# Beginning the first block of an attention kernel by two tiles instead of four

## The reference

```python
xn = layernorm(x)
q = (xn @ Wq + bq) / sqrt(256); k = xn @ Wk + bk; v = xn @ Wv + bv
w = softmax(where(causal, q @ k.T, -inf))
x = x + (w @ v) @ Wo + bo
h = layernorm(x); h_prev = h shifted down by one row, zeros on top
r  = sigmoid((mu_r * h + (1 - mu_r) * h_prev) @ W_r)
kk = relu((mu_k * h + (1 - mu_k) * h_prev) @ W_k) ** 2
out = x + r * (kk @ W_v)
```

## Time and profile before

| | |
|---|---|
| median of 3 executions | 365.44 us (364.97 to 365.71) |
| profiled execution | 365.21 us, of it 363.2 us span |
| TensorE busy (matmuls) | 353.2 us, 97% of the span |
| VectorE, ScalarE, GpSimd busy | 254.8, 239.2, 209.0 us |

### The profile page before, as it was taken

How to read it: one execution, slowest core, us unless ns; L and a number is a source line. 1 busy time by engine, 2 the same in 40 slices (tenths; PEclk the granted TensorE clock), 3 DMA queues, 4 the chain that set the end, 5 groups by cost and what they waited for, 6 DMA issues and landing times.

```text
span 363.2 us, 6783 instructions
## 1 busy us (share of the span) xinstructions
PE 353.2 (97%) x2466; PEld 324.5 (89%) x2466; DVE 254.8 (70%) x569; ACT 239.2 (66%) x467; POOL 209.0 (58%) x246
## 2 busy tenths in 40 slices
PE   8999999999999999999999999999999999999995
PEld 6788888989899888899998989999999999989885
DVE  4597888698946786855568876786857558673645
ACT  2355543987659547597565679587368877789572
POOL 4013330468777743579644357678155768699781
PEclk9999999999999999999999999999999999999999
DMA  7600000000012003003000000030000000000001
GB/s 214 220 2 1 2 0 3 0 3 1 2 38 79 1 0 117 1 2 90 28 3 0 2 0 3 29 88 1 3 29 31 0 3 2 30 31 0 31 29 58
DMA packets 11905, 10.64 MB, mean 29 GB/s; under 512 B 1889, under 2 KB 11874, under 8 KB 11874
## 3 DMA queue, kind: packets, MB, share of 16 engines
q1 hardware_dynamic: 10512, 10.23, 8.8%
q10 hardware_dynamic: 1362, 0.01, 0.2%
HBM read 6.04 MB, written 4.19 MB: 28 GB/s over the span
## 4 chain that ended last, share of the span: by engine, by line
PE 76%; DVE 8%; POOL 6%; ACT 5%; issue 3%; DMA 1%; SPq 0%; ACTq 0%; DVEq 0%
PE W L794 16%; PE W L797 16%; PE W L798 15%; PE O L961 7%; PE O L963 7%; PE O L962 7%; PE W L830 3%; POOL kT_hi L364 3%; DVE mix L710 2%; DVE h_row L696 1%; POOL mix_lo L369 1%; DMA h_row<-in_L_attn_Wq_dram 1%; DVE st L675 1%; ACT mix L471 1%; ACT st L416 1%
## 5 line engine op out<-in xcount | busy, mean ns | idle before, releaser
L364 POOL TENSOR_TENSOR p_lo<-st,p_hi 128x512 fp32r<-128x512 f32 (+1 forms) x71 | 80.9, 1157 | 38.8 <-ACT p_hi L416 37.7
L663 DVE TENSOR_TENSOR peak<-peak,W 128x512 f32<-128x512 f32 (+3 forms) x70 | 42.2, 603 | 47.9 <-ACT st L416 47.7
L416 ACT ACTIVATE st<-W 128x512 f32<-128x512 f32 (+1 forms) x79 | 42.5, 538 | 42.3 <-PE W L798 42.2
L961 PE MATMUL O<-v_hi,p_hi 128*128 128x258 f32 x241 | 69.1, 287 | 0.2 <-DVE x_in L685 0.2
L963 PE MATMUL O<-v_hi,p_lo 128*128 128x258 f32 x241 | 68.0, 282 | 0.0
L962 PE MATMUL O<-v_lo,p_hi 128*128 128x256 f32 x241 | 67.7, 281 | 0.0
L797 PE MATMUL W<-xT_lo,kT_hi 128*128 128x512 f32 (+2 forms) x188 | 65.9, 350 | 0.0
L794 PE MATMUL W<-xT_hi,kT_hi 128*128 128x512 f32 (+2 forms) x188 | 64.4, 343 | 0.8 <-DVE kT_lo L573 0.8
L798 PE MATMUL W<-xT_hi,kT_lo 128*128 128x512 f32 (+2 forms) x188 | 63.2, 336 | 0.0
L452 ACT ACTIVATE st<-st 128x512 f32<-128x512 f32 (+1 forms) x79 | 44.8, 567 | 8.7 <-DVE st L675 8.6
L416 ACT ACTIVATE p_hi<-st 128x512 fp32r<-128x512 f32 (+1 forms) x71 | 40.4, 569 | 15.3 <-PE O L963 13.4
(11 more groups left out here) (138 smaller groups left out, 824.3 us busy)
## 6 DMA issues: line engine op xcount, KB each, us to landing
out_dram<-gate SPq DMA_DIRECT2D x15, 256.0 KB, 2.1
x_in<-in_L_attn_y_all_dram SPq DMA_DIRECT2D x7, 512.0 KB, 4.5
x_in<-in_L_attn_y_all_dram SPq DMA_DIRECT2D x2, 256.0 KB, 4.8
h_row<-in_L_attn_Wk_dram SPq DMA_DIRECT2D x1, 256.0 KB, 3.1
h_row<-in_L_attn_Wq_dram SPq DMA_DIRECT2D x1, 256.0 KB, 4.3
st<-in_L_attn_Wv_dram SPq DMA_DIRECT2D x1, 256.0 KB, 5.3
st<-in_L_attn_Wo_dram SPq DMA_DIRECT2D x1, 256.0 KB, 5.5
mix<-in_L_ffn_W_k_dram SPq DMA_DIRECT2D x1, 256.0 KB, 6.6
```

The source lines that it names most:

```text
L364: g.tensor_tensor(lo[:, r], score_tile(u), hi[:, r].bitcast(f32), ALU.subtract).then_inc(p_split, 1)
L416: a.activation(dst, src, ACT.Copy, **kw).then_inc(done, 1)
L663: v.tensor_tensor(peak[:, J % 2, r], peak[:, J % 2, r], scores, ALU.max).then_inc(maxed, 1)
L961: mm(o[:, 0:VW], hi[:, r], v_hi[:, j + b, :], start=j + b == 0, stop=False)
```

## The change

It touches the start alone (and two counts of semaphores that the slots wait for).

- The layer norm of block 0 releases its first two tiles by themselves: the constant 1 is written, and `xhat_ready` raised, after tile 1 and again after tile 3.
- `first_xT(i)` transposes two tiles of `xhat`, both halves of the channels (4 transposes), into one bank. `first_xT(0)` comes right behind the fold, then Wv's transposes, then `first_xT(1)`.
- `xT_hi` and `xT_lo` of block 0 are written by halves of the queries (256 of them, all channels) instead of by halves of the channels. The size of each instruction stays 128x512.
- The key projection of block 0 is done for 256 queries and then for the other 256: 24 matmuls of 256 columns instead of 12 of 512.
- The fold of `wkq` begins with the first half of its contraction as soon as the first half of `wqT` is there (`q_taken` is raised by each half), and its two halves of the result lie in two banks (`folded`). `wkq_hi` and `wkq_lo` are written as two instructions of 256 columns each instead of one of 512.
- `IDLE` goes from (6, 1, 5, 6, 1) to (6, 1, 3, 0, 0): nine products of zeros fewer.

```diff
-    IDLE = (6, 1, 5, 6, 1)
+    IDLE = (6, 1, 3, 0, 0)
...
+        folded = (bank_b, early[0])
...
             for d in range(KC):
-                last = a.activation(wqT[:, d, 1:C], early[1][:, d * C + 1:(d + 1) * C], ACT.Identity, bias=minus_first[:, d:d + 1])
-            last.then_inc(q_taken, 1)
-
-            sc.wait_ge(fold_ready, 3)
-            high(wkq_hi[:], pairs(bank_b), fold_moved, scale=SCALE)
+                a.activation(wqT[:, d, 1:C], early[1][:, d * C + 1:(d + 1) * C], ACT.Identity, bias=minus_first[:, d:d + 1]).then_inc(q_taken, 1)
+
             for h in range(KC):
-                xT_part(0, h)
+                sc.wait_ge(fold_ready, 3 + h)
+                high(wkq_hi[:, h, :], folded[h][:, 0:C], fold_moved, scale=SCALE)
+            for i in range(2):
+                sc.wait_ge(xT_ready, i + 1)
+                high(xT_hi[:, 0, :, i * 2 * P:(i + 1) * 2 * P], pairs(bank_of("xT", 0, i)), xT_high)
...
-                if t == TG - 1:
-                    dve.wait_ge(xhat_done, TG * (G + 1))
-                    v.memset(xhat[:, :, 0:1], 1.0).then_inc(xhat_ready, 1)
+                if t == TG - 1 or G == 0 and t == 1:
+                    dve.wait_ge(xhat_done, TG * G + t + 1)
+                    v.memset(xhat[:, t - 1 if G == 0 else 0:t + 1, 0:1], 1.0).then_inc(xhat_ready, 1)
...
-            dve.wait_ge(fold_moved, 1)
-            v.scalar_tensor_tensor(wkq_lo[:], bank_b[:].rearrange("p (k c) -> p k c", k=KC), SCALE,
-                                   wkq_hi[:].bitcast(f32), ALU.mult, ALU.subtract).then_inc(fold_split, 1)
             for h in range(KC):
-                xT_part(0, h)
-            taken(early[2], wvT, 4, 1)
+                dve.wait_ge(fold_moved, h + 1)
+                v.scalar_tensor_tensor(wkq_lo[:, h, :], folded[h][:, 0:C], SCALE, wkq_hi[:, h, :].bitcast(f32), ALU.mult, ALU.subtract)                    .then_inc(fold_split, 1)
+            for i in range(2):
+                c = slice(i * 2 * P, (i + 1) * 2 * P)
+                dve.wait_ge(xT_high, i + 1)
+                low(xT_lo[:, 0, :, c], bank_of("xT", 0, i)[:].rearrange("p (k c) -> p k c", k=KC), xT_hi[:, 0, :, c], xT_split)
+            taken(early[2], wvT, 5, 1)
...
+            def first_xT(i):
+
+                pe.wait_ge(xhat_ready, i + 1)
+                for h in range(KC):
+                    for t in range(2):
+                        last = nc.tensor.transpose(bank_of("xT", 0, i)[:, (2 * h + t) * P:(2 * h + t + 1) * P], xhat[:, 2 * i + t, h * P:(h + 1) * P], ident[:])
+                last.then_inc(xT_ready, 1)
+
...
-            pe.wait_ge(q_taken, 1)
-            for h in range(KC):
-                for d in range(KC):
-                    last = mm(bank_b[:, h * C:(h + 1) * C], wkT[:, d, h * P:(h + 1) * P], wqT[:, d, :], start=d == 0, stop=d == KC - 1)
-            last.then_inc(fold_ready, 1)
+            for d in range(KC):
+                pe.wait_ge(q_taken, d + 1)
+                for h in range(KC):
+                    last = mm(folded[h][:, 0:C], wkT[:, d, h * P:(h + 1) * P], wqT[:, d, :], start=d == 0, stop=d == KC - 1)
+                    if d == KC - 1:
+                        last.then_inc(fold_ready, 1)
             idle(IDLE[3])
-            for h in range(KC):
-                xT(0, h)
+            first_xT(0)
             pe.wait_ge(wv_loaded, 16)
             transposed(raw_v, early[2])
+            first_xT(1)
             idle(IDLE[4])
...
-            pe.wait_ge(fold_moved, 1)
-            for w, x, done in ((wkq_hi, xh, xT_high), (wkq_lo, xh, fold_split), (wkq_hi, xl, xT_split)):
-                for k in range(KC):
-                    pe.wait_ge(done, 1 if done is fold_split else k + 1)
-                    for h in range(KC):
-                        last = mm(bank_of("kT", 0, h)[:], w[:, k, h * P:(h + 1) * P], x[:, k, :], start=x is xh and w is wkq_hi and k == 0,
-                                  stop=x is xl and k == KC - 1)
-                        if x is xl and k == KC - 1:
-                            last.then_inc(kT_ready, 1)
+            for i in range(2):
+                c = slice(i * 2 * P, (i + 1) * 2 * P)
+                for w, x, done in ((wkq_hi, xh, xT_high), (wkq_lo, xh, fold_split), (wkq_hi, xl, xT_split)):
+                    for k in range(KC):
+                        if done is fold_split:
+                            pe.wait_ge(done, k + 1)
+                        else:
+                            pe.wait_ge(fold_moved, k + 1)
+                            pe.wait_ge(done, i + 1)
+                        for h in range(KC):
+                            last = mm(bank_of("kT", 0, h)[:, c], w[:, k, h * P:(h + 1) * P], x[:, k, c], start=x is xh and w is wkq_hi and k == 0,
+                                      stop=x is xl and k == KC - 1)
+                            if x is xl and i == 1 and k == KC - 1:
+                                last.then_inc(kT_ready, 1)
```

More of the change, by code:

```diff
@@ L531, in _ @@
             for d in range(KC):
-                last = a.activation(wqT[:, d, 1:C], early[1][:, d * C + 1:(d + 1) * C], ACT.Identity, bias=minus_first[:, d:d + 1])
-            last.then_inc(q_taken, 1)
-            sc.wait_ge(fold_ready, 3)
-            high(wkq_hi[:], pairs(bank_b), fold_moved, scale=SCALE)
+                a.activation(wqT[:, d, 1:C], early[1][:, d * C + 1:(d + 1) * C], ACT.Identity, bias=minus_first[:, d:d + 1]).then_inc(q_taken, 1)
             for h in range(KC):
-                xT_part(0, h)
+                sc.wait_ge(fold_ready, 3 + h)
[3 more added lines that the diff above has]
+                high(xT_hi[:, 0, :, i * 2 * P:(i + 1) * 2 * P], pairs(bank_of("xT", 0, i)), xT_high)
             for h in range(KC):
                 kT_part(0, h)
-            sc.wait_ge(fold_ready, 5)
+            sc.wait_ge(fold_ready, 6)
             high(wvo_hi[:], pairs(early[0]), fold_moved)
@@ L634, in _ @@
                 ln1_apply(0, t)
-            dve.wait_ge(fold_moved, 1)
-            v.scalar_tensor_tensor(wkq_lo[:], bank_b[:].rearrange("p (k c) -> p k c", k=KC), SCALE,
-                                   wkq_hi[:].bitcast(f32), ALU.mult, ALU.subtract).then_inc(fold_split, 1)
             for h in range(KC):
-                xT_part(0, h)
-            taken(early[2], wvT, 4, 1)
+                dve.wait_ge(fold_moved, h + 1)
[5 more added lines that the diff above has]
+            taken(early[2], wvT, 5, 1)
             for h in range(KC):
                 kT_part(0, h)
-            dve.wait_ge(fold_moved, 2)
+            dve.wait_ge(fold_moved, 3)
             low(wvo_lo[:], early[0][:].rearrange("p (k c) -> p k c", k=KC), wvo_hi[:], fold_split)
@@ L831, in transposes @@
                 return last
+            def first_xT(i):
[4 more added lines that the diff above has]
+                last.then_inc(xT_ready, 1)
             def xT(G, h):
                 free("xT", G, h)
-                pe.wait_ge(xhat_ready, G + 1)
+                pe.wait_ge(xhat_ready, G + 2)
                 transposes(bank_of("xT", G, h), xhat, h, range(TG)).then_inc(xT_ready, 1)
@@ L840, in kT @@
                 pe.wait_ge(xT_split, KC * (G + 1))
-                if G == 0:
-                    pe.wait_ge(fold_split, 1)
                 project(bank_of("kT", G, h)[:], wkq_hi, wkq_lo, slice(h * P, (h + 1) * P),
@@ L849, in vv @@
                 if G == 0:
-                    pe.wait_ge(fold_split, 2)
+                    pe.wait_ge(fold_split, 3)
                 by_rows(bank_of("v", G, i), range(2 * i, 2 * i + 2), xT_hi[:, G % NT], xT_lo[:, G % NT], wvo_hi, wvo_lo).then_inc(v_ready, 1)
```

## The result

The changed kernel takes 363.27 us (median of 4, 363.17 to 363.32) beside 365.56 us for the kernel before (median of 4, 364.97 to 365.71): ratio 0.994, 95% interval 0.9923 to 0.9957, so faster by 0.4 to 0.8%. Its profiled execution took 363.31 us with a span of 361.2 us, against 365.21 and 363.2. The gain is about 2.0 us by the spans and 2.3 us by these medians; 1.0 was forecast. In the later comparisons, with 21 to 25 executions each, the kernel before has medians of 365.28 to 365.33, and against those the gain is 2.0 us too.

A forecast was written before the change was run, and what follows sets the result against it. The prediction took TensorE's chain (76% of 363.2 us) as the bound, its start set by the second constant write at 10.49. The wvo fold 1.0 us earlier, with the rest sliding along: 365.44 - 1.0 = 364.4 us, range 363.9 to 365.3.

The forecast's parts named there:

- The true bound of the start: Start: the second write of the constant, ending at 10.49 us, bounds it; the change leaves what it hangs on as is.
- Transposes, switch, projection: Behind the second write: transposes from 10.60, switch to split matmuls 0.10, projection 24 x 0.118 = 2.83 us; wvo fold from 13.89.
- The waits: Five places in the new start could wait; only the ninth projection matmul, for xT_lo, was charged: 0.05 us.
- The sum for the start: The fold of wvo begins 14.97 - 13.92 - 0.05 = 1.0 us earlier, bounds 0.75 to 1.1.
- The clock: Rival: TensorE's clock falls back between 9 and 11 us, projection 2.4 us longer, 366.8 us; chance 0.08.
- "Worth nothing" for the fold by halves: Start: fold by halves, 3 zeros instead of 5 and two ACT instructions gain nothing, since the work on x covers them.
- The step that failed: Everything behind the start, vector-bound parts too, should slide by the same 1.0 us, giving span 362.2 us.

The follow-up runs named there:

- e8: The changed kernel with the key projection of block 0 as 12 matmuls of 512 columns again: 364.17 us, ratio to before 0.9971.
- e1: The changed kernel with the wkq fold, wkq_hi and wkq_lo whole as before, so as many scalar-engine instructions as before: 364.26 us, ratio to before 0.997.
- e10: e1 plus one scalar-engine activation of 128x2 behind kT_hi of the start: 363.18 us, ratio to before 0.9945.
- e3: The kernel before plus one scalar-engine activation of 128x2 behind kT_hi of the start: 364.24 us, ratio 0.9971.
- e14: The kernel before plus one scalar-engine activation of 128x2 in slot 40, at 151.4 us: 365.40 us, ratio 1.0003.
- e2: The kernel before plus a GpSimd memset of 128x4 in front of the mix_lo that met the norm: 365.69 us, ratio 1.0006.
- e4: The kernel before with only IDLE changed to (6, 1, 3, 0, 0), fewer zeros: 365.19 us, ratio 1.0002.
- e5b: e5 run again (the kernel before, GpSimd waiting for the norm at 126 us): 364.56 us, ratio 0.9985.
- e6: The changed kernel with IDLE = (6, 1, 5, 6, 1) as before, the nine zeros put back: 364.32 us, ratio to before 0.9973.
- e12: The changed kernel with the vector engine adding the epsilon for block 0 instead of GpSimd: 363.47 us, ratio to before 0.9954.
- e5: The kernel before with GpSimd waiting until the norm at 126 us is done before its mix_lo: 364.49 us, ratio 0.9979.

## Why the prediction was right about its place and wrong about its size

**The true bound of the start: right.** The second constant write bounds it. It ended at 10.68, not 10.49, since in this execution the first pair was normed 0.20 us later (8.80 against 8.60). The first matmul of the transposes was forecast 0.11 behind its end and came 0.06 behind it (10.74). The later write is not of the change: the first statistics of x start at 6.59 in this trace and at 6.38 in the one of before, but at 6.40 in e8 and 6.66 in e1, which have the same order up to there.

**Transposes, switch, projection: right.** From that matmul to the fold of `wvo` I had 13.92 - 10.60 = 3.32 us; it is 14.06 - 10.74 = 3.32. Inside, the switch cost 0.08 (a first step of 0.20 in the place of 0.12; I had 0.10), the step is 0.118 us, and the last transpose came 0.38 behind the first, not 0.33.

**The waits: right.** No hole before the ninth matmul (I had put 0.05). `wkq_lo` in two ran 10.60 to 11.35, 0.75 us where I had 0.87 of bounds 0.68 and 0.87. `wvT` ended at 13.73, 0.33 ahead of the fold of `wvo`; forecast was 0.3.

**The sum for the start: right, its closeness in part luck.** 0.91 us against 1.0, with bounds 0.75 to 1.1. The path from the end of the second write to the fold of `wvo` took 3.38 us, and I had 3.48 with the wait; the write came 0.19 later than in my sum. With the write at the same time the gain would be 1.10, at the upper bound. e1 has 0.82 in its profile and 1.0 in the median.

**The clock: the rival did not happen.** The steps in the projection are 0.118 us, the 2.4 GHz level's, and the granted clock from 11.16 to 14.06 is 1.00, with a fold and then 1.4 us of nothing but transposes ahead of them. The rule of the Trainium skill that I had weighed ("TensorE: Matmul & The Clock Gate", Part 4: PE-mode transpose) speaks of transposes that do not count as busy in the way that matmuls do. These rows show no fall behind these twelve transposes, and deny nothing about more.

**"Worth nothing" for the fold by halves: right for what it does, wrong for what it issues.** In the start it is worth nothing: e10 without it is as fast. But it adds a scalar-engine instruction, and that one is worth 1.0 us at 122 to 131 us (e1 against the changed kernel and e10; e3 by itself).

**The step that failed:** "So the whole rest, its vector-bound parts too, should slide by the same 1.0 us. The tables of slots are an order, not times." It does slide when only times change (e1). It does not when an engine's stream of instructions gets longer, since the scalar engine is late by 0.28 us at a position in its stream, and whether VectorE's norm starts at the same moment as GpSimd's `mix_lo` (within 0.01 us) or 0.21 us ahead of it hangs on that, and is worth 1.06 us to TensorE. The forecast looked at no row beyond 21 us, though the page of the profile of before gives 0.8 us of idle time to `kT_lo` at line 794, all of it one wait and the second longest of TensorE behind the start (the longest is 0.9 us, at 79.08). Following that wait would have found the norm of 1.45 us, and with it a rival on the far side of the range: the gain with the lock-out gone, 365.44 - 1.0 - 1.06 = 363.4 us.

**What stays open.** Why the scalar engine is late at that position is inferred; no run separates it. The number of packets on the profile's instruction queue q8 does not follow it: 19 in the kernel before (late) and in e3 (not late), 20 in the kernel after (not late) and in e14 (late). The time of one packet on q14 does, the other queue of the kind "instruction", with 12 packets of 8 KB in a span. The two late instructions of the kernel before, at 122.48 and 189.65, are exactly 128 records of the scalar engine apart, its waits counted. By the trace's DMA records one of the q14 packets starts 0.64 to 0.92 us behind the start of `mix_hi` in the six traces in which `mix_hi` is late (123.14 in the kernel before; e1, e2, e4, e5b, e14), and 3.3 to 3.4 us ahead of it in the six in which it is not (117.92 in the kernel after; e3, e6, e8, e10, e12). There it falls in a wait of the scalar engine for TensorE, 1.35 us from 117.12 on in the kernel after. The Trainium skill ("Runtime: NRT & Kernel Launch", Instruction fetch mechanics) says that instructions are fetched in blocks and that crossing into the next one is mostly hidden. These packets fit a crossing into the next block that one more instruction moves out of a busy stretch into a wait. That the fetch is what holds the engine up is still an inference.

## What to carry to other kernels

An edit that issues one instruction more or less on some engine is not free because it is hidden: everything behind it in that engine's stream takes another position, and here one 0.3 us delay decided whether two engines met. Before forecasting that the rest slides, read the largest waits of TensorE in the whole profile, find which of them hang on two engines that start within some 0.3 us of each other, and put their price beside the forecast as a rival. When a gain is twice what the edited lines explain, add one empty instruction to the old kernel before crediting the edit.

## What the runs showed of the hardware

- A VectorE norm of 128x256 from SBUF to SBUF takes 0.41 us. It took 1.45 to 1.49 where GpSimd's `mix_lo` of 1.3 us started between 0.002 us ahead of it and 0.04 us behind it (before, e1, e2, e4, e14), and ended 0.15 us behind the end of `mix_lo` each time. Where it started 0.21 us or more ahead (the kernel after, e3, e5b, e6, e8, e10, e12), it took 0.41.
- The scalar engine started one instruction 0.28 us late with nothing in the trace to wait for. Another instruction in front of it in the stream (e3, e10) took the delay away from there, one behind it (e14) did not, but took away a later one of 0.17 us.
- Twice, in e1 and in e5, a single execution took some 1960 us instead of 364. In the profile of e5's the matmuls of 512 columns follow each other at 1.28 us, 5.6 times the 0.229 us of the earlier trace rows, while the granted clock is given as 1.00. They are in none of the ratios, and without them the two medians are 0.03 us lower. Timeline of that execution, TensorE:

```profile
58.60 1.62 PE L1019 MATMUL W<-xT_hi,wkq_lo 128*128 128x512 f32 x1
59.88 1.62 PE L1019 MATMUL O<-xT_hi,wkq_lo 128*128 128x512 f32 x1
```
